# Both chunks of the value products in the even slots, the other TensorE events in the odd slots

## What is computed

```
x = x + tanh(g_xattn) * attention(layernorm(x), ctx)      # 16 heads of 8 channels, 256 x 256 scores, softmax
x = x + tanh(g_ffn)   * ffn(layernorm(x))                 # 256 -> 1024 -> 256

q = Wq @ target + bq ; k = Wk @ source + bk ; v = Wv @ source + bv
dot = mask * (q.T @ k / sqrt(8)) - (1 - mask) * 1e6 ; amap = softmax(dot) * mask ; out = amap @ v.T

# ffn: activations rounded to 8 bits by the row's largest absolute value, weights to -1, 0, 1 by their mean
h = silu(bitlinear(y, W1)) ; bitlinear(h, W2)
```

## Time and profile before

| | us |
|---|---|
| median of 3 runs | 223.91 (220.95 to 225.38) |
| profiled execution | 222.08 |
| its span, first to last instruction | 219.7 |
| mean granted TensorE clock | 0.969 of full |

### The profile page before, as it was taken

The page is one execution under the profiler, slowest core; times in us unless marked ns, Lnnn a source line. Parts: engine busy times, 40 slices in busy tenths (PEclk is TensorE's granted clock), DMA queues, the critical chain, the costliest instruction groups (busy, mean ns, idle before and its releaser), DMA issues.

```text
span 219.7 us, 5141 instructions
## 1 busy us (share of the span) xinstructions
PE 183.4 (83%) x1994; PEld 110.7 (50%) x2008; DVE 138.3 (63%) x276; ACT 118.1 (54%) x167; POOL 88.2 (40%) x155
## 2 busy tenths in 40 slices
PE   6997479856888689889899998988989888999854
PEld 6765234423645345455465554464546454646742
DVE  2597343543675839765987687579766962632863
ACT  2334044847488855575446646654573566566141
POOL 6393694200031460840186428203810470083151
PEclk9999557999999999999999999999999999999999
DMA  4439204883000102200001024000000000000001
GB/s 129 71 116 284 90 0 134 139 118 114 3 3 3 21 1 48 51 1 4 0 4 21 4 47 98 3 30 0 4 0 28 0 4 0 28 0 0 27 1 48
DMA packets 8407, 9.23 MB, mean 42 GB/s; under 512 B 1516, under 2 KB 6828, under 8 KB 8380
## 3 DMA queue, kind: packets, MB, share of 16 engines
q1 hardware_dynamic: 7576, 8.52, 16.1%
q10 hardware_dynamic: 808, 0.40, 0.9%
HBM read 5.66 MB, written 1.05 MB: 31 GB/s over the span
## 4 chain that ended last, share of the span: by engine, by line
PE 48%; DVE 16%; ACT 14%; POOL 8%; issue 7%; DMA 6%; ACTq 1%; POOLq 0%; DVEq 0%
PE ps_exp L1041 23%; ACT probs L579 8%; DVE nmx L749 6%; DMA q<-negm 6%; PE ps_pv L1057 5%; PE ps_max L1068 3%; PE ps_max L1126 3%; PE ps_max L931 2%; PE ps_exp L913 2%; PE ps_max L1034 2%; PE ps_exp L1116 2%; DVE hb L797 1%; PE ps_exp L911 1%; PE ps_exp L1103 1%; DVE hs L802 1%
## 5 line engine op out<-in xcount | busy, mean ns | idle before, releaser
L749 DVE TENSOR_REDUCE nmx<-ps_max 128x2 f32<-128x512 f32 x122 | 78.5, 686 | 39.0 <-PE ps_max L1034 38.9
L579 ACT ACTIVATE probs<-ps_exp 128x1024 f32<-128x1024 f32 x64 | 65.4, 1024 | 56.4 <-PE ps_exp L1041 55.7
L1041 PE MATMUL ps_exp<-q,k 32*128 32x256 f32 x512 | 75.1, 410 | 20.0 <-DVE nmx L749 8.6
L1034 PE MATMUL ps_max<-k,q 32*128 32x256 f32 x488 | 71.7, 412 | 1.5 <-POOL q L340 1.2
L1041 PEld LDWEIGHTS ps_exp<-q,k 32*128 32x128 f32 x512 | 47.6, 190 | 42.2 <-issue 20.3
L1034 PEld LDWEIGHTS ps_max<-k,q 32*128 32x128 f32 x488 | 43.2, 190 | 2.5 <-POOL q L340 1.7
L1057 PE MATMUL ps_pv<-probs,v_aug 128*32 128x256 f32 x512 | 40.9, 391 | 0.0
L321 POOL TENSOR_SCALAR rstd<-mv 128x1 f32<-128x1 f32 (+1 forms) x13 | 3.0, 227 | 80.2 <-DVE mv L785 75.2
L797 DVE SCALAR_TENSOR_TENSOR hb<-hb,ps_exp 128x512 f32<-128x512 f32 x14 | 9.5, 681 | 19.7 <-ACT hb L634 19.5
L1057 PEld LDWEIGHTS ps_pv<-probs,v_aug 128*32 128x32 f32 x512 | 10.1, 108 | 21.0 <-issue 20.7
L400 POOL TENSOR_TENSOR qk<-qk,mask_b 128x512 f32<-128x512 f32 (+1 forms) x8 | 9.1, 1138 | 18.4 <-ACT qk L544 18.1
(11 more groups left out here) (159 smaller groups left out, 235.6 us busy)
## 6 DMA issues: line engine op xcount, KB each, us to landing
w_nat<-in_L_ffn_W SPq DMA_DIRECT2D x8, 256.0 KB, 5.8
out<-x_sb SPq DMA_DIRECT2D x8, 128.0 KB, 1.8
c_sb<-in_ctx SPq DMA_DIRECT2D x3, 256.0 KB, 9.9
mask_b<-in_mask_Bx1x_fk SPq DMA_DIRECT2D x1, 768.0 KB, 7.5
k<-qk SPq DMA_DIRECT2D x12, 64.0 KB
q<-qk SPq DMA_DIRECT2D x12, 64.0 KB
x_sb<-in_x SPq DMA_DIRECT2D x1, 512.0 KB, 8.9
x_sb<-in_x SPq DMA_DIRECT2D x2, 128.0 KB, 3.3
```

The source lines that it names most:

```text
L579: nc.scalar.activation(probs[:, s % PROBS, :], ps_exp[:, exp_at[("exp", s)] % 2, :], ACT.Exp).then_inc(S["exp_done"], 1)
L749: nc.vector.tensor_reduce(max_columns(g, hh), ps_max[:, at % VEC, :].rearrange("t (c s) -> t c s", c=DC), AX_X, ALU.max, negate=True).then ...
L1034: return nc.tensor.matmul(bank[:, c * T:(c + 1) * T], at_rows(q4, b, h)[:, c * 128:(c + 1) * 128], at_rows(k4, b, h), start=True, stop=True)
L1041: return nc.tensor.matmul(bank[:, o:o + T], at_rows(k4, b, h)[:, c * 128:(c + 1) * 128], at_rows(q4, b, h), start=True, stop=True)
```

## The change

```diff
-        PAIR_EVENTS = {"fixed": -10, "stats": -10, "xn": -9, "k": -8, "rows_k": -7, "q": -6, "rows_q": -5}
+        PAIR_EVENTS = {"fixed": -10, "stats": -10, "xn": -9, "k": -10, "rows_k": -9, "q": -6, "rows_q": -5}
...
-        ENTRY_EVENTS = {"att": 10, "back": 11, "y_max": 14, "y_quant": 14, "y_turn": 16, "upa": 17, "ha": 17, "ra": 18,
-                        "upb": 19, "hb": 19, "rb": 20, "h_quant": 20, "h_turn": 23, "down": 25}
-
-        LAST_EVENTS = {"att": 10, "back": 11, "y_max": 12, "y_turn": 12, "upa": 15, "ha": 15, "ra": 15, "upb": 15, "hb": 15,
+        ENTRY_EVENTS = {"att": 9, "back": 11, "y_max": 13, "y_quant": 13, "y_turn": 15, "upa": 17, "ha": 17, "ra": 17,
+                        "upb": 19, "hb": 19, "rb": 19, "h_quant": 20, "h_turn": 23, "down": 25}
+
+        LAST_EVENTS = {"att": 9, "back": 11, "y_max": 12, "y_turn": 12, "upa": 15, "ha": 15, "ra": 15, "upb": 15, "hb": 15,
                        "rb": 15, "h_quant": 15, "h_turn": 18, "down": 19}
...
-                if 2 <= s < SLOTS + 2:
-                    attend(s // 2 - 1, s % 2)
+                if 2 <= s < SLOTS + 2 and s % 2 == 0:
+                    attend(s // 2 - 1, 0)
+                    attend(s // 2 - 1, 1)
```

## The result

The changed kernel takes 242.92 us (median of 4 runs, 241.94 to 252.53), the kernel before 224.64 beside it; the ratio is 1.0988 (95% interval 1.0925 to 1.1051). The profiled execution took 243.07 us with a span of 240.7, against 222.08 and 219.7: 21.0 us more. The ratio is larger than 242.92 / 224.64 = 1.081, as it leaves out executions over 1.5% above the fastest of their kernel (252.53 here, and at least 225.38 and 226.44 before); against 221.61 to 221.91, the medians of the kernel before in the later comparisons, 242.92 would be about 1.095.

What follows compares the result with a forecast made beforehand. Quiet slots were taken as bound by a latency loop through VectorE, event slots by TensorE or VectorE. 3.7 + 1.2 + 7.75 + 1.7 = +14.3 on 222.1 gave 236.4 (238.2 by the median); 237 us was taken, range 229 to 243.

Steps and rivals of the forecast that it cites:

- The bound: Quiet slots: a 2.06 us latency loop through VectorE, attend free inside it; event slots bound by TensorE or VectorE.
- Part 1: Pairing the attends: sixteen instructions cost 1.00 us (0.86 to 1.14); the possible 8.3 us saving stays hidden behind the maxima.
- Part 2: Moved events, slots 16 to 55: plain turn 22.22 against 20.47 us; five turns +7.75 us (+5 to +10).
- The wait for the copy: Slot 1 of a turn: att waits for ACT's pv copy, TensorE stands 1.2 us; slot 4.87 instead of 3.67.
- Part 3: Start: k and its rows two slots earlier delay the weight loads; slot 8 is +3.7 us (+1.7 to +6).
- shift DMA 2, issued behind exp 5, lands by then: Start: the DMA that slot 8 needs lands in time for slot 8 at 54.3 us (half clock).
- Part 4: Slots 8 to 15: k, the second weight turn and y meet in slot 15; +1.2 us (0 to +3).
- Part 5: The end: late y of entry 6, the pv copy and the absolute maximum cost +1.7 us (0.5 to +3).
- Rivals A: TensorE's change-overs decide and VectorE's latency gives way: 213.8 us; chance 0.05.
- B: The start costs nothing but the turns do: 227.6 to 232.8 us; chance 0.16.
- C: Saved attends pay for the copy wait and VectorE delays: within 2%, 219.5 to 228 us; chance 0.09.
- Rival D: Cold clock for most of slots 5 to 15, sixteen attend instructions at 1.14: 243 to 250 us; chance 0.10.

Runs made afterwards that it cites:

- y back: The changed kernel with y_max, y_quant and y_turn at their old offsets 14, 14, 16 again: ratio 1.0825 to the kernel before, median 239.27 us.
- att early alone: The kernel before with the attends paired and only att moved, to offset 9: ratio 1.0283 to the kernel before, median 227.65 us.
- k back: The changed kernel with k and rows_k of all pairs at their old places (-8, -7): ratio 1.0707 to the kernel before, median 236.63 us.
- maxima back: The changed kernel with the absolute maxima ra, rb at 18 and 20 again: ratio 1.0653 to the kernel before, median 236.49 us.
- rows_k back: The changed kernel with rows_k at -7 again and k left early at -10: ratio 1.0879 to the kernel before.

## Why the prediction was right or wrong

**The bound.** Right in what it said of the gain: the pairing brought none. Its picture was too simple. The loop through VectorE is that of the even slot 6 of a turn, which with both attends is now bound by TensorE at 2.07. A quiet odd slot, of which the prediction said that it would wait about 0.9 for the row maxima, is not in a turn at all, as slots 1, 3, 5 and 7 all hold an event; what held the odd slots was the row maxima in slot 3 (a wait of 0.95) and ACT's exp in slots 5 and 7 (0.79 and 0.60).

**Part 1.** Right to 0.01: sixteen instructions take 1.00, and the even slot 2.07 to 2.08. The rule that a change of tiling mode drains TensorE (the Trainium skill, "TensorEngine Tiling (Array Packing)", Key Properties) agrees with this, as one change-over fewer makes sixteen instructions 0.14 shorter than twice 0.57; here the time was waited away.

**Part 2.** Right slot by slot (table above), with 22.22 predicted and 22.19 measured at full clock. Slots 16 to 55 grew by (199.60 - 83.69) - (180.58 - 74.05) = 9.4 us, 7.75 predicted; 1.64 of the difference is slot 54. There the granted clock fell to half from the slot's start:

```profile
193.00:197.00 4.00, 3.92 (x36) 1.89 (x40) 2.02 (x4) 1.57 (x4) 2.88 (x6) 0.57 0.02 6
```

Before it fell TensorE had waited 0.75 and 0.79 us at the starts of slots 53 and 54. The prediction had reckoned with a cold clock only at the start. The four other turns grew by 1.49, 2.32, 0.62 and 1.60, in sum 6.0, as four times 1.5 had it; that the single ones lie so far apart makes this sum in part luck.

What the prediction did not say is which of its terms were dear. The wait for the copy is the most visible, but slots 2 and 3 are shorter for it, and at full clock a turn with att early is not longer. The absolute maxima ahead of the row maxima (6.4 us by the medians) and turn y (3.7 us, 2.1 of it in slot 15) are what costs.

**Part 3.** The chain was right link by link: the mask ahead of the clearing, at 28.17 (27.3 predicted), the clearing 3.8 later (3), loads at 40.4 (39.4), w_sum 0 at 46.2 (45.5), a wait of TensorE of 7.1 us (8 and more), half clock behind it. The size was not: slot 8 at 56.2, +5.7 instead of +3.7. The step that failed is "shift DMA 2, issued behind exp 5, lands by then". Its issue on ACT's queue in the kernel after:

```profile
49.70 0.54 ACTq L622 DMA_DIRECT2D q<-negm  x1
```

and in the kernel before:

```profile
44.00 0.55 ACTq L622 DMA_DIRECT2D q<-negm  x1
```

Slot 8 followed at 56.23, 6.5 us after the issue, having waited 1.88 for it; without this wait it would have started at 54.35, where the prediction had it (54.3). Before it had followed at 50.57, 6.6 after the issue. I had taken the DMA to land within 4.6 us, though the trace of before showed 6.6. Other executions of such kernels show that this time is not fixed (last section), so that it was late is shown, and why is not.

**Part 4.** The other failed term: slots 8 to 15 grew by (83.69 - 56.23) - (74.05 - 50.57) = 4.0, not 1.2. Slot 15 alone went from 3.75 to 6.00 (+2.25), by the weight copy on ACT that slot 16's bank needs: the mechanism that the prediction had, put at half its size. With y moved back the slot is 3.87, so y makes 2.1 of it and k next to nothing. Slots 8 and 9 went from 4.59 to 7.30 (+2.7). Of this 1.1 is att of the first entry, now in slot 9, and slot 10 gives it back; the kernels with the absolute maxima or y back, which have the same att there and full clock, need 5.71. The other 1.6 is half clock, which the prediction had left out, as its cold stretch ended at slot 8.

**Part 5.** +2.0 against +1.7.

**Sum.** 5.7 + 4.0 + 9.4 + 2.0 = 21.0 against 14.3. Of the missing 6.7 us, 2.0 are the shift DMA and the start, 2.8 slots 8 to 15, 1.6 the fall of the clock in slot 54, 0.3 the end. Rivals A, B and C fell. Rival D's cold clock came only in part of slots 5 to 9, not for most of slots 5 to 15, and without its dearer attends. The chance for slower, 0.86, was fair; the upper end at 243 left too little for falls of the clock.

## What to carry to other kernels

Before taking instructions off the busiest engine, look whether the slot ends by its work or by a loop of latency through another engine; in the second case the freed time turns into idle time. When an event is moved in a schedule that all engines share, walk each engine's queue past it: here a projection of 2 us was put into idle time of TensorE, and slot 8 came 8 us later all the same, because its mask stood ahead of a clearing for which the weight loads waited (57.35 against 49.33, both kernels with the attends paired). And behind every new stall, ask which DMA was issued behind it and how long the last one of its kind took, and whether the clock will still be full.

## What the runs showed of the hardware

The granted clock fell to half in the middle of a busy stretch, behind waits of only 0.75 to 1.2 us of TensorE, and not each time. Slot 57 shows it best, as six traced kernels with paired attends have the same wait of 1.18 us for the copy in it: in three the clock fell (att early alone, k back, maxima back), in three it did not (the changed kernel, y back, rows_k back). Such a fall cost 1.6 to 1.7 us, in slot 54 of the changed kernel too. In the kernel before no fall is seen from 36 us to the last slots, neither behind waits of 0.90 and 1.06 (the start and the middle of slot 15) nor behind the one of 3.29. What decides is open.

The small shift DMA (8 KB), issued among the weight loads, has no fixed time. From its issue to the start of slot 8 it was 6.6 us before and 6.5 after; in the other traces with k at its old place or the clearing early it was 3.7 to 4.9 us, and in those with k early and the clearing late 5.6 to 7.2, and 9.1 with rows_k back. What it waits for on the way was not traced.
